# A decoder's two cross attentions: the transposition of the row maxima, and ScalarE's copy of it, one head earlier in the order

## What is computed

```
qh = q.reshape(B, 8, 16, 256);  kh = k.reshape(B, 8, 16, 256);  vh = v.reshape(B, 8, 16, 256)
qk  = einsum('bhdq,bhdl->bhql', qh, kh) / sqrt(16)
sm  = softmax(qk, axis=-1)                    # 256 queries x 256 keys, per item and head
ret = einsum('bhql,bhdl->bhdq', sm, vh).reshape(B, 128, 256)
x   = layernorm(x + gamma * ret)              # keys and values are ctx_2048 in both
```

## Time and profile before

| | |
|---|---|
| median of 3 runs | 1439.13 us (1437.67 to 1444.99) |
| profiled execution | 1438.84 us, its span 1437.1 us |
| mean granted TensorE clock over the span | 0.904 |
| cross attention ca0, `shifted(0, 0)` to the last item | about 272 to 425 us of the span |
| cross attention ca1, likewise | about 1142 to 1295 us |
| PE busy over the span | 1139.4 us, 79% |
| DVE / ACT / POOL busy over the span | 915.0 / 558.5 / 492.5 us |

### The profile page before, as it was taken

One profiled execution on the slowest core, in us unless ns is written; L12 is line 12 of the kernel. 1 busy time (PEld: TensorE's weight loads), 2 busy tenths in 40 slices (PEclk: granted clock), 3 DMA queues, 4 the chain that ended last, 5 costly groups with the idle time before them and its releaser, 6 DMA issues. The chain is left out here.

```text
span 1437.1 us, 31266 instructions
## 1 busy us (share of the span) xinstructions
PE 1139.4 (79%) x9497; PEld 883.2 (61%) x9568; DVE 915.0 (64%) x2406; ACT 558.5 (39%) x1306; POOL 492.5 (34%) x971
## 2 busy tenths in 40 slices
PE   4599998599964353345999999999999599986997
PEld 4466675366641122125998899898988366654665
DVE  3488995477758999982444444444445378765886
ACT  3245554266642121122323332333233166653553
POOL 5276886233322222221232233223223223322232
PEclk8889999699996667667999999999999699998999
DMA  7899995434424011001010010001001234431111
GB/s 152 176 183 225 189 168 114 115 115 122 128 75 93 23 33 33 25 22 63 12 38 23 29 33 25 22 29 37 22 19 34 83 116 128 124 89 49 55 51 41
DMA packets 145419, 111.84 MB, mean 78 GB/s; under 512 B 17872, under 2 KB 131840, under 8 KB 145344
## 3 DMA queue, kind: packets, MB, share of 16 engines
q1 hardware_dynamic: 132032, 100.01, 28.4%
q10 hardware_dynamic: 11344, 8.72, 2.2%
q0 software_dynamic: 1968, 2.16, 0.9%
HBM read 68.91 MB, written 31.52 MB: 70 GB/s over the span
## 5 line engine op out<-in xcount | busy, mean ns | idle before, releaser
L388 DVE TENSOR_REDUCE ca_nm<-ca_p_s 128x2 f32<-128x512 f32 x256 | 170.5, 686 | 79.4 <-PE ca_p_s L296 72.6
L522 ACT ACTIVATE ca_pt<-ca_p_e 128x512 f32<-128x512 f32 x256 | 152.0, 597 | 89.7 <-PE ca_p_e L318 88.2
L296 PE MATMUL ca_p_s<-ca_ks,ca_qs 96*128 96x256 bf16 x512 | 103.7, 288 | 41.5 <-DMA ca_ks<-k_stack 37.2
L316 PE MATMUL ca_p_e<-ca_qs,ca_ks 96*128 96x256 bf16 x512 | 130.3, 280 | 0.2
L318 PE MATMUL ca_p_e<-ca_mt,row_of 96*128 96x256 bf16 x512 | 129.0, 278 | 0.0
L2064 ACT ACTIVATE la_pq<-la_p_s,la_nm 128x128 f32<-128x128 f32 x256 | 73.2, 369 | 106.2 <-DVE la_nm L2104 106.2
L1897 PE MATMUL la_p_f<-la_qt,q_w 128*128 128x128 f32 x512 | 101.4, 280 | 12.5 <-ACT la_lt L2045 11.3
L1555 PE MATMUL mx_p_i<-identb,mx_qi 128*128 128x128 bf16 x128 | 19.4, 307 | 108.8 <-POOL mx_qi L1406 108.8
L1898 PE MATMUL la_p_f<-la_qt,q_w 128*128 128x128 f32 x512 | 99.0, 275 | 0.0
L296 PEld LDWEIGHTS ca_p_s<-ca_ks,ca_qs 96*128 96x128 bf16 x512 | 45.3, 101 | 69.2 <-DMA ca_ks<-k_stack 30.1
L1897 PEld LDWEIGHTS la_p_f<-la_qt,q_w 128*128 128x128 f32 x512 | 77.6, 192 | 16.3 <-ACT la_lt L2045 16.3
(11 more groups left out here) (282 smaller groups left out, 3009.6 us busy)
## 6 DMA issues: line engine op xcount, KB each, us to landing
sa_qks<-sa_qkp SPq DMA_DIRECT2D x96, 128.0 KB, 4.9
ca_qs<-q_stack SPq DMA_DIRECT2D x64, 192.0 KB, 2.9
ca_ks<-k_stack SPq DMA_DIRECT2D x64, 192.0 KB, 3.2
ca_ct<-in_ctx_t SPq DMA_DIRECT2D x32, 128.0 KB, 3.0
ca_xr<-x_state SPq DMA_DIRECT2D x32, 128.0 KB, 2.1
x_state<-ca_xn SPq DMA_DIRECT2D x32, 128.0 KB, 2.7
k_stack<-sa_cxp SPq DMA_DIRECT2D x16, 192.0 KB, 2.8
q_stack<-sa_parts SPq DMA_DIRECT2D x16, 192.0 KB, 2.6
```

The lines of the kernel that those rows point to most:

```text
L296: last = pe.matmul(p_s[h % 2][:, qc, :], QS[u][:, h, 128 * qc:128 * qc + 128], KS[u][:, h, :], start=True, stop=True)
L316: pe.matmul(p_e[h % 2][:, kc, :], KS[u][:, h, 128 * kc:128 * kc + 128], QS[u][:, h, :], start=True, stop=False)
L388: dve.tensor_reduce(NM[u][:, h, :], p_s[h % 2][:, :, :], AX.X, ALU.max, negate=True).then_inc(max_done, 1)
L522: act.activation(PT[h // 4][:, h % 4, :, :], p_e[h % 2][:, :, :], ACT.Exp, scale=SCALE).then_inc(exp_done, 1)
```

## The change

Two instructions' places are moved, each by one head, on two engines. On TensorE `turn_max` of item b's group 1 goes from before `shifted(b, 3)` to before `shifted(b, 2)`, and `turn_max` of item b+1's group 0 from before `shifted(b, 7)` to before `shifted(b, 6)`, which also puts it ahead of `scores(b+1, 6)` and `turn_back(b-1)`. On ScalarE `copy_max` of group 1 goes from behind `exps(b, 2)` to behind `exps(b, 1)` and the copy of the output, and that of item b+1's group 0 from behind `exps(b, 6)` to behind `exps(b, 5)`. No instruction is added or removed, and no wait or count is changed. The code ahead of the pairs (L349 to L352, L530) stays as it is.

```diff
@@ -357,9 +357,9 @@
                     later = follow(i, u)
                     first = isinstance(b, int) and b == 0
                     for h in range(H):
-                        if h == 3:
+                        if h == 2:
                             turn_max(i, u, 1)
-                        if h == 7 and later:
+                        if h == 6 and later:
                             turn_max(*later, 0)
                         shifted(i, u, h)
                         if later:
@@ -537,9 +537,9 @@
                         exps(i, u, h)
                         if h == 1 and not (isinstance(b, int) and b == 0):
                             copy_out(b - 1)
-                        if h == 2:
+                        if h == 1:
                             copy_max(i, u, 1)
-                        if h == 6 and later:
+                        if h == 5 and later:
                             copy_max(*later, 0)
```

## The result

The changed kernel takes 1448.58 us (median of 14 runs, 1444.29 to 1456.28), the kernel before 1441.13 us on the same chips (14 runs, 1435.49 to 1448.66). The ratio is 1.0057, 95% interval 1.0038 to 1.0076: 5.5 to 11 us slower, 8.2 us in the middle. The forecast was 7.9 us slower.

The account below looks back on a forecast made before the run. A closed loop through last scores, L409 and queued loads bounds the kernel; 6.2 lateness + 1.0 handoff + 0.9 restart - 0.2 = +7.9 us on 1438.84 gives 1446.7, forecast as 1447.0 us for the median, range 1440.5 to 1451.

Parts of the forecast that it names:

- The waits for the copy are not in the loop: TensorE's 4.4 us of waits lie outside the loop of last scores, reduction, L409, queued loads, keys, heads 4 to 7.
- 6.2 us of latenesses: At head 6 group 0's transposition input comes 0.01 us early to 0.55 late, 6.2 us over 26 iterations.
- 0.9 us for the restart: After a stop the next weight load may not start under the second transposition's: 0.035 us each, 0.9 over 26.
- All of it goes into the period: Whatever is lost or gained between the fourth head and the last scores goes into the iteration's length in full.
- Group 1: nothing: Group 1's move before head 2 costs zero: input ready 0.4 us early, ScalarE's delay covered by head 4's wait.
- what is gained in heads 0 to 3 is only waited for at the fourth: Time gained before head 4 does not shorten the iteration, since TensorE then waits for the keys.
- The weight load that might pass the held transposition: `shifted(b, 6)` could load weights during the stop, giving back 2.6 us over 26; none taken.
- The -0.2 us of the sum: Gain from the earlier copy, 0.1 us in iteration 0 of each stage, where no loop runs yet.
- The sign that I had named: L306 waits for L482 in about 26 places, some 7 us; `shifted` waits for L515 all but vanish.
- The second rival: TensorE stops, but loop slack gives half back: +3 to +4 us, 1442 to 1443; chance 0.27.
- the third: Group 1's copy ahead of `exps(b, 2)` delays the value product or head 4: 3 to 5 us more; chance 0.06.
- The fourth: The order is rearranged on the way to the chip, so the change does nothing: 1439; chance 0.01.

Follow-up runs that it names:

- e6: Changed kernel with the residual's load moved behind the second half of keys and the context's load in SyncE's queue; ratio 0.9898 to the kernel before.
- e1: Kernel before with only group 0's transposition and copy moved one head ahead, group 1's left where they were; ratio 1.0074.
- e3: Changed kernel with the context's load issued right behind the first half of queries and keys; ratio 0.9996 to the kernel before.
- e4: Kernel before with the context's load issued right behind the first half of queries and keys; ratio 1.000.
- e5: Kernel before with the residual's load moved behind the second half of keys and the context's load in SyncE's queue; ratio 0.9899.
- e8: Kernel before with group 0's transposition, before head 7, done three times over, four more matmuls per item; ratio 1.0043.
- e2: Kernel before with only group 1's transposition and copy moved one head ahead, group 0's left where they were; ratio 1.001.
- e9: Kernel before with group 1's transposition, before head 3, done three times over, four more matmuls per item; ratio 1.0018.

## Why the prediction was right

**The waits for the copy are not in the loop.** Right. They went from 4.4 to 1.0 us and the time did not fall, not even in e6 with no load awaited.

**6.2 us of latenesses, taken from before, one iteration at a time.** Right. After the change the stops were 2.8 and 3.9 us, 6.7 us, with a handoff of 0.05 in each, so 5.4 us of lateness in place of 6.2, and 1.3 of handoff in place of 1.0. The lateness of a given iteration was not repeated (iteration 7 had 0.49 and then 0.37); it hangs on how the loads land. The sum carries over only roughly: in e1 it is 7.1 us.

**0.9 us for the restart.** The size was right and the reason wrong. Behind the stop the next weight load comes 0.10 us after L306's first, sooner than the 0.16 of before, so there is no slow restart. The 0.03 us is there with no stop too (e3 against e4, e6 against e5), as a price of the new order, and arises behind `shifted(b, 7)`.

**All of it goes into the period.** Right: the cut loop grew by 0.256 and 0.322 us, 7.5 us over 26 iterations, and e8 shows that work on this side of the wait for keys counts in full. The sum had 8.1 us for these iterations; their periods grew by 7.8.

**Group 1: nothing.** Right (e2), but the reason is the wait for VectorE before `scores(b+1, 3)`, and not that head 4's wait for keys covers it. That what is gained in heads 0 to 3 is only waited for at the fourth is wrong in the same way: TensorE waits for it at head 3 already. **The weight load that might pass the held transposition: no gain taken.** Right in effect: in iteration 7 L316's first load follows L306 by 0.10 us (346.62 after 346.52), and in no iteration does it stand before it.

**What agreed by chance.** Iteration 0 was 0.9 us shorter in both stages of the profile after, where I had 0.1. Kernels with the unchanged order have 8.66 to 10.04 us there (before, e4, e5): its mean clock there is 0.68 and 0.66 in the profile before and 0.74 and 0.72 after, so it is when the clock rises, not the change. The -0.2 us of the sum can't be read there. Iteration 1, at full clock, is 0.10 us shorter where group 0 has moved (8.31 after 8.41 and 8.40), and item 15 0.09 longer (6.67 and 6.66 after 6.58), which cancel. The rest of the span was 2.4 us longer in the same profile, and it varies from 1144 to 1153 us over these kernels, whose other stages are all alike. The two cancel in part, and the 8.3 us between the two spans is no proof of the sum; the iterations are. The median of 14 runs, +8.2 us by the ratio, is.

**The sign that I had named** was half wrong: I foretold some 7 us of waits of L306 in 26 places, and the view shows 34.9 us in 73, because it also books the drain of `weigh`, 0.41 us at a time.

The second rival (slack that gives half back) and the third (ScalarE's order) fall with e8 and e2: e8 finds no slack on this side of the keys, and e2 no loss, in item 15 either (6.58 and 6.59 us). The fourth, an unchanged program, falls with the rows.

## What to carry to other kernels

Before an instruction on an in-order engine is moved ahead of work that is ready, subtract its new place from the end of its producer, one iteration at a time: here these differences, 0.01 us early to 0.55 late, came to 6.2 us, most of a loss of 8.2, while the wait to be removed (4.4 us) was off the loop. Find the loop first, by asking which wait ends last: here a DMA queue behind one small VectorE operation bounded an engine that looked 95% busy, and turning two loads round was worth nearly twice what this change lost (some 15 against 8.2 us). And ask of each test which wait took its work in: e9 came out as expected, for another reason than the expected one.

## What I had not expected of the hardware

Stops of about 2 us in each iteration took TensorE's granted clock to 0.86 or 0.87 in 16 of 26 iterations and to 0.75 in one, while nine with stops as long kept 1.00; this cost some 30 us beyond the stops themselves, of 84 in all; stops of up to 0.56 us left it at 1.00. A transposition of a 128 x 96 bf16 tile in a row of its like costs 0.06 us, half of the 0.11 that I took from the 256-column matmuls beside it.
